# Deeper rings for the x loads of a recurrent layer and its feed-forward block, and one load moved to the GpSimd queue

## The reference, cut to what matters

```python
xn = layernorm(x)                                    # x: 4 x 4096 x 2048
Bu = xn @ (gamma*B).T                                # complex, 256 states
h_t = A * h_(t-1) + Bu_t                             # complex scan over time
s  = Re(H @ C.T) + D * xn
routed = sigmoid(xn @ w_router + b) > 0.5
h1 = rmsnorm(xn);  v = h1 @ wv + bv;  h = xn + v @ wo
h2 = rmsnorm(h);   mlp = (silu(h2 @ w_gate) * (h2 @ w_up)) @ w_down
ffn = where(routed, h + mlp, xn)
out = x + s * silu(ffn)
```

## Time and profile before

| what | us |
|---|---|
| median of 2 runs | 3672.14 (3669.3 to 3674.97) |
| the profiled execution, its time | 3667.75 |
| its span on the slowest core (core 3) | 3666.2 |
| spans of the other cores | 3649.5 to 3662.3 |
| mean granted TensorE clock, cores | 0.868 to 0.875 |
| PE busy, DVE busy, ACT busy | 2689.2, 1152.0, 382.1 |

### The profile page before, as it was taken

One profiled execution on the slowest core, in us unless ns is written; L12 is line 12 of the kernel. 1 busy time (PEld: TensorE's weight loads), 2 busy tenths in 40 slices (PEclk: granted clock), 3 DMA queues, 4 the chain that ended last, 5 costly groups with the idle time before them and its releaser, 6 DMA issues.

```text
span 3666.2 us, 31484 instructions; the slowest of 8 cores (3649.5 to 3666.2 us)
## 1 busy us (share of the span) xinstructions
PE 2689.2 (73%) x11744; PEld 1145.3 (31%) x11744; DVE 1152.0 (31%) x1489; ACT 382.1 (10%) x459; POOL 363.6 (10%) x311
## 2 busy tenths in 40 slices
PE   6131243339848999998788872985799999878887
PEld 1000111114313444443333330432344444433333
DVE  1546456462450100012333434045101000133334
ACT  2122000021120000000000002112100000000000
POOL 0000000001101111111000100110111111100010
PEclk9666686769979999999889995997899999989999
DMA  6032342456867787786777765786777877688676
GB/s 184 23 122 85 110 123 80 108 104 65 127 154 76 74 81 73 77 81 74 98 116 107 100 101 113 74 118 139 94 77 73 81 75 75 73 111 120 101 103 101
DMA packets 736952, 354.76 MB, mean 97 GB/s; under 512 B 683530, under 2 KB 685594, under 8 KB 732061
## 3 DMA queue, kind: packets, MB, share of 16 engines
q0 software_dynamic: 679728, 178.28, 49.6%
q1 hardware_dynamic: 57074, 174.46, 15.5%
HBM read 497.34 MB, written 33.61 MB: 145 GB/s over the span
## 4 chain that ended last, share of the span: by engine, by line
PE 58%; DMA 21%; DVE 12%; issue 4%; ACT 2%; PEld 1%; DVEq 1%; PEldq 1%; POOL 0%; ACTq 0%; SPq 0%; POOLq 0%
PE ps L153 58%; DMA arena<-down_p 9%; DVE arena L157 5%; DMA arena<-xT 4%; DMA arena<-xNB 3%; DVE arena L177 2%; ACT arena L174 2%; DMA arena<-wv_p 2%; PEld ps L153 1%; DMA arena<-wo_p 1%; DMA arena<-up_p 1%; DVE arena L161 1%; DVE arena L169 1%; DVE small L157 1%; PEldq L187 1%
## 5 line engine op out<-in xcount | busy, mean ns | idle before, releaser
L153 PE MATMUL ps<-arena 128*128 128x512 bf16 x11264 | 2550.6, 389 | 661.4 <-DMA arena<-down_p 201.0
L153 PEld LDWEIGHTS ps<-arena 128*128 128x128 bf16 x11264 | 1113.0, 100 | 2097.4 <-issue 854.8
L157 DVE TENSOR_TENSOR arena<-arena,ps 128x512 bf16<-128x512 f32 (+1 forms) x304 | 209.0, 687 | 1264.6 <-ACT arena L174 1121.9
L157 DVE TENSOR_TENSOR arena<-arena,m_bc 128x512 f32<-128x512 f32 (+1 forms) x128 | 122.7, 959 | 746.0 <-PE ps L153 456.6
L174 ACT ACTIVATE arena<-arena 128x512 f32<-128x512 f32 (+4 forms) x135 | 146.8, 1088 | 1436.0 <-DVE arena L181 897.2
L174 ACT ACTIVATE arena<-ps 128x512 f32<-128x512 f32 x176 | 105.2, 597 | 1095.4 <-PE ps L153 1082.8
L147 POOL DMA_DIRECT2D arena<-gate_p x88 | 100.6, 1143 | 1125.3 <-PE ps L153 993.9
L157 DVE TENSOR_TENSOR arena<-arena 128x512 f32<-128x512 f32 (+8 forms) x227 | 187.5, 826 | 45.0 <-DMA hspill<-arena 14.2
L153 PE MATMUL ps<-arena,ones_bf 128*1 128x512 bf16 x256 | 80.4, 441 | 157.5 <-DVE arena L177 147.1
L177 DVE CAST arena<-arena 128x1024 bf16<-128x1024 f32 (+1 forms) x96 | 83.7, 872 | 275.1 <-DMA arena<-xT 134.8
L147 POOL DMA_DIRECT2D arena<-down_p x64 | 85.9, 1343 | 783.6 <-PE ps L153 783.6
(11 more groups left out here) (49 smaller groups left out, 378.5 us busy)
## 6 DMA issues: line engine op xcount, KB each, us to landing
arena<-xT SPq DMA_DIRECT2D x96, 512.0 KB, 4.9
arena<-gate_p POOLq DMA_DIRECT2D x88, 512.0 KB, 6.3
arena<-up_p POOLq DMA_DIRECT2D x88, 512.0 KB, 8.1
arena<-down_p POOLq DMA_DIRECT2D x64, 704.0 KB, 9.7
arena<-xT SPq DMA_DIRECT2D x16, 1024.0 KB, 5.0
arena<-xNB SPq DMA_DIRECT2D x16, 1024.0 KB, 5.3
arena<-xNB SPq DMA_DIRECT2D x32, 512.0 KB, 4.8
arena<-wv_p POOLq DMA_DIRECT2D x32, 512.0 KB, 6.4
```

Source lines behind the costliest of these rows:

```text
L153: E.matmul(o, l, r, start=a, stop=b), inc=inc)
L157: E.tensor_tensor(o, a, b, al), inc=inc)
```

## The change

All blocks of x now go through a ring of four 8 KB slots (`xring`: at 64, 72, 112 and 120 KB), each with a semaphore of its own. The statistics passes use all four, with the waits taken apart: the load waits for the slot's cast (and, in the own pass, its f32 matmuls); the cast waits for the square and the bf16 matmuls that read the bf16 copy of two blocks before; the square waits for the matmuls of two blocks before. The Bu passes and `phase3` use three slots; in `phase3` the third is at 132 KB, and `t3` goes to 84 KB. Since slots 2 and 3 lie at 112 and 120 KB, `pAT` goes to 32 KB, and the spreading of the neighbour mean waits until all that DVE has issued before, the reciprocal among it, is done. The row copy of line 370 signals another semaphore. In `phase6` the load of h is issued by POOL, after both half weight blocks, and waits there for the epilogue; the load of x stays with SP. Each fence waits for two more semaphores.

```diff
-    sX = [mksem("sX0"), mksem("sX1")]
+    sX = [mksem("sX0"), mksem("sX1"), mksem("sX2"), mksem("sX3")]
-    xb = [arF(64 + 8 * i, T) for i in range(2)]
+    xring = [arF(64, T), arF(72, T), arF(112, T), arF(120, T)]
@@ stats_pass
         for k in range(NK):
-            sl = k % 2
-            wait("sync", sV, xslot_v.get(sl))
-            wait("sync", sT, xslot_t.get(sl))
-            mk_x = dma("sync", sX[sl], xb[sl], src[k * 128:(k + 1) * 128, :])
+            sl = k % 4
+            sb = k % 2
+            wait("sync", sV, ring_v.get(sl))
+            wait("sync", sT, ring_t.get(sl))
+            mk_x = dma("sync", sX[sl], xring[sl], src[k * 128:(k + 1) * 128, :])
             wait("vector", sX[sl], mk_x)
-            mkv[k] = xslot_v[sl] = cp("vector", xbf[sl], xb[sl], inc=sV)
+            wait("vector", sS, xbf_sc.get(sb))
+            wait("vector", sT, xbf_tm.get(sb))
+            mkv[k] = ring_v[sl] = cp("vector", xbf[sb], xring[sl], inc=sV)
             wait("scalar", sV, mkv[k])
-            mk_sq = act(xsq[sl], xbf[sl], AF.Square, inc=sS)
+            wait("scalar", sT, xsq_tm.get(sb))
+            mk_sq[k] = xbf_sc[sb] = act(xsq[sb], xbf[sb], AF.Square, inc=sS)
             if own:
-                    mm(ps[q][0:2, :], sw_sb[:, 2 * k:2 * k + 2],
-                       xb[sl][:, q * 512:(q + 1) * 512], k == 0, k == NK - 1)
+                    ring_t[sl] = mm(ps[q][0:2, :], sw_sb[:, 2 * k:2 * k + 2],
+                                    xring[sl][:, q * 512:(q + 1) * 512],
+                                    k == 0, k == NK - 1,
+                                    inc=sT if q == 3 else None)
@@ powers of A
-    pAT = arF(112, T)
+    pAT = arF(32, T)
-    mk_s1 = dma("sync", sH[0], row_S1[0:1, :], row2[1:2, :])
+    mk_s1 = dma("sync", sSm, row_S1[0:1, :], row2[1:2, :])
@@ spreading of the neighbour rows
-    wait("sync", sV, mk_m)
+    wait("sync", sV, sV.v)
     bcast(rowm, mnb_bc)
     wait("sync", sV, mk_rnb)
     bcast(row_sx2[0:1, :], rnb_bc)
@@ bu_pass
-                sl = k % 2
-                wait("sync", sV, xslot_v.get(sl))
-                mk_x = dma("sync", sX[sl], xbh[sl],
+                sl = k % 3
+                sb = k % 2
+                wait("sync", sV, ring_v.get(sl))
+                mk_x = dma("sync", sX[sl], xring[sl][:, 0:TS],
@@ phase3
-    xb3 = [arF(64, TS), arF(68, TS)]
-    t3 = arF(72, TS)
+    t3 = arF(84, TS)
+    xb3c = arF(132, TS)
+        p3buf = [(xring[0][:, 0:TS], sX[0]), (xring[1][:, 0:TS], sX[1]),
+                 (xb3c, sX[3])]
-            if k >= 2:
-                wait("sync", sV, mk_t3u[k - 2])
+            if k >= 3:
+                wait("sync", sV, mk_t3u[k - 3])
@@ phase6
             if d >= 1:
                 wait("sync", sV, mk_ep[2 * d - 1])
+                wait("gpsimd", sV, mk_ep[2 * d - 1])
             for q in range(2):
-                mk_h[q] = dma("sync", sH[q], p6h[q],
+                mk_h[q] = dma("gpsimd", sH[q], p6h[q],
```

More of the change, by code:

```diff
@@ L102, in build_nc @@
     ENG_SEM = {"tensor": sT, "vector": sV, "scalar": sS, "gpsimd": sG}
-    DMA_SEMS = (sSm, sBc, sX[0], sX[1], sH[0], sH[1], sWv[0], sWv[1],
-                sUp[0], sUp[1], sDn[0], sDn[1], sO, sBr, sOut[0], sOut[1])
+    DMA_SEMS = (sSm, sBc, sX[0], sX[1], sX[2], sX[3], sH[0], sH[1],
+                sWv[0], sWv[1], sUp[0], sUp[1], sDn[0], sDn[1], sO, sBr,
+                sOut[0], sOut[1])
     prog = {e: [] for e in ENGINES}
@@ L225, in build_nc @@
                   Bcat.ap().rearrange("k p c -> p k c"))
-    xb = [arF(64 + 8 * i, T) for i in range(2)]
+    xring = [arF(64, T), arF(72, T), arF(112, T), arF(120, T)]
     xbf = [arB(80 + 4 * i, T) for i in range(2)]
     xsq = [arB(88 + 4 * i, T) for i in range(2)]
+    ring_v = {}
+    ring_t = {}
+    bf_t = {}
+    xbf_sc = {}
+    xbf_tm = {}
+    xsq_tm = {}
     row2 = arF(32, T)
@@ L233, in build_nc @@
     row_tmp = arF(56, T)
-    xslot_v = {}
-    xslot_t = {}
     def stats_pass(src, own):
@@ L240, in stats_pass @@
         mkt = {}
+        mk_sq = {}
         for k in range(NK):
-            sl = k % 2
-            wait("sync", sV, xslot_v.get(sl))
-            wait("sync", sT, xslot_t.get(sl))
-            mk_x = dma("sync", sX[sl], xb[sl], src[k * 128:(k + 1) * 128, :])
+            sl = k % 4
[3 more added lines that the diff above has]
+            mk_x = dma("sync", sX[sl], xring[sl], src[k * 128:(k + 1) * 128, :])
             wait("vector", sX[sl], mk_x)
-            mkv[k] = xslot_v[sl] = cp("vector", xbf[sl], xb[sl], inc=sV)
+            wait("vector", sS, xbf_sc.get(sb))
+            wait("vector", sT, xbf_tm.get(sb))
+            mkv[k] = ring_v[sl] = cp("vector", xbf[sb], xring[sl], inc=sV)
             wait("scalar", sV, mkv[k])
-            mk_sq = act(xsq[sl], xbf[sl], AF.Square, inc=sS)
+            wait("scalar", sT, xsq_tm.get(sb))
+            mk_sq[k] = xbf_sc[sb] = act(xsq[sb], xbf[sb], AF.Square, inc=sS)
             if own:
@@ L257, in stats_pass @@
                 for q in range(4):
-                    mm(ps[q][0:1, :], ones_bf[:, :],
-                       xbf[sl][:, q * 512:(q + 1) * 512], k == 0, k == NK - 1)
-            wait("tensor", sS, mk_sq)
+                    mk_nbx = mm(ps[q][0:1, :], ones_bf[:, :],
+                                xbf[sb][:, q * 512:(q + 1) * 512],
+                                k == 0, k == NK - 1,
+                                inc=sT if q == 3 else None)
+                xbf_tm[sb] = mk_nbx
+            wait("tensor", sS, mk_sq[k])
             for q in range(4):
                 mkt[k] = mm(ps[4 + q][0:1, :], ones_bf[:, :],
-                            xsq[sl][:, q * 512:(q + 1) * 512], k == 0, k == NK - 1,
+                            xsq[sb][:, q * 512:(q + 1) * 512], k == 0, k == NK - 1,
                             inc=sT if q == 3 else None)
-            xslot_t[sl] = mkt[k]
+            xsq_tm[sb] = mkt[k]
         return mkt[NK - 1]
@@ L424, in build_nc @@
     cp("vector", small[0:1, C_T1:C_T1 + 1], ps[5][0:1, 0:1])
-    wait("vector", sH[0], mk_s1)
+    wait("vector", sSm, mk_s1)
     wait("vector", sBr, sBr.v)
@@ L476, in build_nc @@
     upl = [arF(8 * i, T) for i in range(4)]
-    xbh = [arF(112 + 4 * i, TS) for i in range(2)]
     xbf_s = [arB(136 + 2 * i, TS) for i in range(2)]
@@ L489, in bu_pass @@
             for k in range(NK):
-                sl = k % 2
-                wait("sync", sV, xslot_v.get(sl))
-                mk_x = dma("sync", sX[sl], xbh[sl],
+                sl = k % 3
+                sb = k % 2
+                wait("sync", sV, ring_v.get(sl))
+                mk_x = dma("sync", sX[sl], xring[sl][:, 0:TS],
                            src[k * 128:(k + 1) * 128, c0:c0 + TS])
                 wait("vector", sX[sl], mk_x)
-                wait("vector", sT, xslot_t.get(sl))
-                xslot_v[sl] = cp("vector", xbf_s[sl], xbh[sl], inc=sV)
-                wait("tensor", sV, xslot_v[sl])
+                wait("vector", sT, bf_t.get(sb))
+                ring_v[sl] = cp("vector", xbf_s[sb], xring[sl][:, 0:TS], inc=sV)
+                wait("tensor", sV, ring_v[sl])
                 for pl in range(4):
@@ L502, in bu_pass @@
                                             k * 512 + (pl + 1) * 128],
-                                    xbf_s[sl][:, q * 512:(q + 1) * 512],
+                                    xbf_s[sb][:, q * 512:(q + 1) * 512],
                                     k == 0, k == NK - 1,
                                     inc=sT if (pl == 3 and q == 1) else None)
-                xslot_t[sl] = mkt[k]
+                bf_t[sb] = mkt[k]
             wait("vector", sT, mkt[NK - 1])
@@ L602, in phase3 @@
         mk_t3u = {}
+        p3buf = [(xring[0][:, 0:TS], sX[0]), (xring[1][:, 0:TS], sX[1]),
+                 (xb3c, sX[3])]
         for k in range(NK):
-            sl = k % 2
-            if k >= 2:
-                wait("sync", sV, mk_t3u[k - 2])
-            mk_x = dma("sync", sX[sl], xb3[sl], xT[k * 128:(k + 1) * 128, c0:c0 + TS])
-            wait("vector", sX[sl], mk_x)
+            sl = k % 3
+            buf, bsem = p3buf[sl]
+            if k >= 3:
+                wait("sync", sV, mk_t3u[k - 3])
+            mk_x = dma("sync", bsem, buf, xT[k * 128:(k + 1) * 128, c0:c0 + TS])
+            wait("vector", bsem, mk_x)
             if k >= 1:
                 wait("vector", sS, mk_h1[k - 1])
-            mk_t3u[k] = tt("vector", t3, xb3[sl], m_bc[:, c0:c0 + TS],
+            mk_t3u[k] = tt("vector", t3, buf, m_bc[:, c0:c0 + TS],
                            AL.subtract, inc=sV)
```

## The result

| | us |
|---|---|
| kernel before, median of all executions (see below) | 3674.4 (3673.5) |
| changed kernel, median of all executions (see below) | 3619.0 (3616.7) |
| ratio, with its 95% interval | 0.9857 [0.9836, 0.9878] |
| the profiled execution of the changed kernel | 3636.95 |
| its span on the slowest core (core 3), on the others | 3635.4, 3586.6 to 3613.7 |

The change brings 0.0143 x 3674 = 53 us, against the 85 of the forecast. Both medians lie above the range (3568 to 3616), the one in brackets by less than 1 us.

A forecast was written before the change was run, and what follows sets the result against it. PE was taken as the main bound (58% of the chain), with 7% waiting for x, which the change goes at. Terms summed to -85.6 us from 3667.75, giving 3582, or 3587 against the median; 8-in-10 range 3568 to 3616.

The forecast's parts named there:

- Own statistics: Statistics of the core's own x: four slots keep the next block ready, blocks 4.29 us apart, -14.5 us.
- Neighbour statistics: Statistics of the neighbour's x: four loads under way, 3.1 us per block, first to last cast 46.5 instead of 78.0, -31.5.
- Spreading: Spreading of the neighbour mean, no longer hidden under the reciprocal; the second spreading waits for the first: +6.2 us.
- Bu passes: Four half passes over x: a third slot takes each from about 44.0 to 34.0 us, -40 in all.
- phase3: With a third slot block 2 no longer waits for x: -3.5 and -1.3 in the two sub-blocks, together -4.8 us.
- phase6: Moving the load of h to POOL costs 0; less competition with weights at each sub-block's start gives -1.5 us in all.
- Rival C: Slower: POOL, held up by loads of h in phase6, delays the weights: 3737 us; chance 0.03.
- rival A: Streams find a lower limit: neighbour blocks at 3.73 us, Bu blocks at 2.4, 3612 us; chance 0.19.
- B: The pace of loads does not rise at all; the deeper ring only queues: 3658 us; chance 0.06.

The follow-up runs named there:

- Experiment 1: Changed kernel with all first-use waits of the statistics passes taken out (a missing note writes no wait): 3594.8 us, ratio to the kernel before 0.9773.
- Experiment 7: Changed kernel with two slots instead of four in the neighbour statistics, waits still taken apart: no time could be given.
- experiment 4: Changed kernel with the neighbour mean spread early again, as before the change: 3620.7 us, one run.
- Experiment 6: Changed kernel with two slots instead of three in the Bu passes: 3658.3 us, one run.
- experiment 10: Same kernel as experiments 8, run again in more rounds: 3563.3 us, ratio to the kernel before 0.9724.
- experiments 8: Changed kernel with the edits of Experiment 1 and experiment 4, and the row copy of line 370 moved behind the neighbour statistics: 3572.3 us, mean of two runs.

## Why the prediction was wrong, point by point

**Own statistics: the step that failed.** "With four slots the next block is always there, so blocks follow at 4.29" was read from the depth of the ring, not from what SP waits for. The true sum: block 4 starts at 61.77, where it started at about 37.24 + 2 x 4.96 = 47.2 before, +14.6; eleven more blocks at 4.64 instead of 4.96, -3.5; together +11.1, as measured (+11.0). The row that would have told was there before the change. The timeline of SP, us 18 to 45 of the kernel before:

```profile
21.68 20.42 SPq L147 DMA_DIRECT2D arena<-xT  x4
```

The first of these is load 1, into a second slot that was empty from the start, and it was issued at 21.68, when PE had done block 0. I took PE's 8.53 us before block 1 for a slow start, and never asked why SP waited. In the same way the diff has a wait on `xbf_tm` in a pass that never sets it, and the code of `wait` says what that means. Experiment 1 is the test: without the fallback this stage ends at 81.1, and even below the forecast of 89.5 (104.0 - 14.5), because load 1 is freed as well. "A gain above 15 has no place to come from" was wrong too, for the same reason: it is 22.9.

**Neighbour statistics: right.** 46.5 between the first and the last cast where 15 x 3.1 = 46.5 was forecast, the DMA share 0.93, PE's granted clock 0.85 on the mean, and 1.00 from 250 us on (core 3). Between the casts at 244.74 and 278.24 of core 3 a block takes 33.50/11 = 3.05 us. The Trainium skill's 358 GB/s for each core of a pair (HBM Reference, Specifications) made it 2.93, and the trace agrees within some 4%. Experiment 7 adds what the forecast had not parted: the depth alone is the smaller share.

**Spreading: right.** +6.4 against +6.2, and experiment 4 takes it back.

**Bu passes: right in mechanism, and in size but for the first.** From the write of the last row to the scan and from there to `phase4`, the difference is -38.1 instead of -43.5. The half passes take 35.9, 35.2, 33.8 and 34.5 us (medians over the cores; 39.0 for the first on core 3) where 34.0 was forecast. The first carries the third place of the fallback, as DVE's timeline shows (changed kernel, core 3; the casts of blocks 1 and 2):

```profile
419.64 1.48 DVE L178 CAST arena<-arena 128x1024 bf16<-128x1024 f32 x2 [3.87 <-PE ps L154]
```

With it gone (experiment 1) the first half takes 32.5, and the neighbour's part gains 20.1 of the 20 forecast. Experiment 6 gives the third slot 39 us.

**phase3: right.** Block 2 finds its x: 1.44 us, the usual turn, where it waited 4.92 before. So it is on all eight cores and in both sub-blocks. The forecast's 3.5 was read from core 3; in s = 0 block 2 had waited for x on five of the eight cores only (3.3 to 6.0 us), and on the other three there was nothing to gain.

```profile
695.59 1.23 DVE L158 TENSOR_TENSOR arena<-arena,m_bc 128x1024 f32<-128x1024 f32 x1 [1.44 <-ACT arena L175]
```

**phase6: right in that the move costs nothing.** Rival C did not occur, by 10.5 us or more of slack in every block. The small gain of 1.5 that was added is not shown by any run.

**The rivals and the range.** The time is near that of rival A (3612), but A's mechanism is not there: neighbour blocks at 3.1 and not 3.73, Bu half passes at 35 and not 38. All the rivals were about sizes, limits and queues; none said that a part of the change might not do what it seems to, because a wait is wider than its name. With the own statistics as forecast, 25.5 us less, the time would have been some 3591 and inside; the one term with a wrong sign put it outside.

**What stays open.** From `phase4` to the end there are two sub-blocks of nearly the same work in all kernels, and the medians over the cores lie between 2808 and 2825 us in eleven profiles, with no order by kernel. So does an earlier start reach the end? In single profiles part of it seems lost: in experiment 1 `phase4` starts 36 us sooner than in the changed kernel and the median core ends 23 us sooner. But the kernel before, too, differs by 9 us on the median core between the executions beside experiment 1 and those beside experiment 10 (3661.2 and 3652.3). Against the executions of the kernel before that ran beside it, the median core ends 86.7 us sooner in experiment 1, and 102.3 and 100.5 in experiments 8 and 10, where `phase4` starts 89.7, 105.6 and 106.1 sooner. With a standard error of 2 to 3 us each, nearly all of it arrives. Whether the last few us are lost stays open, and a single profile can't resolve experiment 4's 6 us.

## What to carry to other kernels

A deeper ring is only as deep as the waits in front of its loads: before counting slots, find on the timeline of the queue that issues the loads when each of the first ones goes out, and what it waited for. Where a list of instructions is written out in program order by helpers, read what a missing note means; "wait for all so far" is safe and silent, and its price grows with the number of slots. A term that comes out of "it is always there" deserves a rival of its own.

## What the runs showed of the hardware that was not expected

A single load got twice as slow while the stream got faster. In the neighbour statistics a load of 1 MB takes 10.6 us to land in the changed kernel against 5.3 before, and yet blocks come every 3.1 us instead of 5.2; in the Bu passes 6.0 instead of 4.8 us, at 2.2 us per block instead of 2.9 (second half pass, casts of blocks 4 and 15 at 480.38 and 504.88: 24.50/11). The list of issues of the changed kernel:

```profile
arena<-xNB SPq DMA_DIRECT2D x16, 1024.0 KB, 10.6
arena<-xNB SPq DMA_DIRECT2D x32, 512.0 KB, 6.0
```

The forecast had said that single loads stretching in step with their number would speak for rivals A or B. Counted in slots, the 1 MB loads did just that: twice the slots, twice the time. But the slots before were not always loading. From the time of a load and the pace one can estimate how many were in flight: 5.3/5.2 = 1.0 before and 10.6/3.1 = 3.4 after, in the Bu passes 4.8/2.9 = 1.7 and 6.0/2.2 = 2.7. What counts is whether a load stretches more than the number in flight grows, and the pace has to be read from the casts.
